# A fused four-layer cross-attention kernel: the Mamba block's heads computed with channels on partitions, its squares summed on TensorE, and the batches' stages merged in another order

## The reference, cut to what matters

```python
zxbcdt = _rms(x, norm_w) @ in_proj_w
z = zxbcdt[..., :D_INNER]                       # D_INNER = 512
xBC = zxbcdt[..., D_INNER:D_INNER + CONV_DIM]   # 768 channels
dt = jax.nn.softplus(zxbcdt[..., -H_M:] + dt_bias)
...                                             # conv over 4 taps, then silu
xh = xBC[..., :D_INNER].reshape(b, L, H_M, HEADDIM)   # 8 heads of 64
...                                             # scan over the tokens gives ys
y = ys.transpose(1, 0, 2, 3) + D_skip[None, None, :, None] * xh
u = _rms(y.reshape(b, L, D_INNER) * jax.nn.silu(z), gnorm_w)
return resid + u @ out_proj_w
```

## Time and profile before

| | |
|---|---|
| median of 3 runs | 1412.81 us (1411.97 to 1413.31) |
| the profiled execution | 1414.21 us |
| its span, first to last instruction | 1411.0 us |
| mean granted clock of TensorE | 0.956 |
| TensorE busy with products | 1261.4 us, 89% |
| TensorE busy with weight loads | 996.6 us, 71% |
| VectorE | 959.5 us, 68% |
| ScalarE | 783.4 us, 56% |
| POOL | 339.1 us, 24% |

### The profile page before, as it was taken

The page is one execution under the profiler, slowest core; times in us unless marked ns, Lnnn a source line. Parts: engine busy times, 40 slices in busy tenths (PEclk is TensorE's granted clock), DMA queues, the critical chain, the costliest instruction groups (busy, mean ns, idle before and its releaser), DMA issues.

```text
span 1411.0 us, 25836 instructions
## 1 busy us (share of the span) xinstructions
PE 1261.4 (89%) x9426; PEld 996.6 (71%) x9426; DVE 959.5 (68%) x1877; ACT 783.4 (56%) x2690; POOL 339.1 (24%) x766
## 2 busy tenths in 40 slices
PE   3567889999999999999999999999999999988755
PEld 2345667877787887877787778788787778766633
DVE  2355466969687877868696968777786869583522
ACT  1124364857565666757475756566675847464411
POOL 0101313231322232232323132223223232302020
PEclk9779999999999999999999999999999999999755
DMA  6901010100001010101000000101010100000000
GB/s 200 331 1 41 1 42 1 34 16 19 29 0 48 0 48 0 45 4 45 4 25 23 15 33 0 48 0 48 0 45 4 45 4 11 27 5 4 4 4 4
DMA packets 28586, 44.38 MB, mean 31 GB/s; under 512 B 4710, under 2 KB 20614, under 8 KB 28044
## 3 DMA queue, kind: packets, MB, share of 16 engines
q1 hardware_dynamic: 26252, 31.41, 7.0%
q0 software_dynamic: 2304, 12.58, 2.5%
HBM read 37.65 MB, written 6.34 MB: 31 GB/s over the span
## 4 chain that ended last, share of the span: by engine, by line
PE 64%; DVE 21%; ACT 11%; issue 2%; DMA 1%; POOL 1%; SPq 0%; POOLq 0%; DVEq 0%; ACTq 0%
PE psum L487 43%; PE psum L481 7%; ACT A L790 5%; ACT sa_p L790 4%; DVE small_ L1003 4%; PE psum L642 3%; PE psum L535 3%; PE psum L694 2%; PE psum L706 2%; PE psum L661 2%; DVE A L997 2%; DVE sa_p L1011 1%; DVE sa_p L997 1%; PE psum L551 1%; DVE A L1088 1%
## 5 line engine op out<-in xcount | busy, mean ns | idle before, releaser
L1279 POOL TENSOR_SCALAR small_<-small_ 128x1 f32<-128x1 f32 x112 | 37.1, 331 | 865.3 <-ACT A L908 382.5
L790 ACT ACTIVATE A<-A,small_ 128x128 f32<-128x128 f32 x384 | 148.6, 393 | 86.0 <-DVE small_ L1004 86.0
L481 PE MATMUL psum<-cst,A 128*128 128x128 f32 x672 | 108.3, 288 | 64.4 <-DVE A L1011 27.0
L783 ACT ACTIVATE A<-psum 128x1024 f32<-128x1024 f32 (+2 forms) x112 | 77.1, 688 | 156.9 <-PE psum L481 109.1
L481 PEld LDWEIGHTS psum<-cst,A 128*128 128x128 f32 x672 | 80.3, 147 | 101.4 <-DVE A L1011 40.5
L1168 DVE SCALAR_TENSOR_TENSOR A<-psum,half_cw,A 128x127 f32<-128x127 f32 (+2 forms) x288 | 75.2, 343 | 41.1 <-ACT A L894 41.1
L790 ACT ACTIVATE sa_p<-sa_p,small_ 128x128 f32<-128x128 f32 x256 | 99.1, 397 | 4.4 <-DVE small_ L1004 4.4
L790 ACT ACTIVATE ca_p<-ca_p,small_ 128x128 f32<-128x128 f32 x256 | 98.7, 391 | 4.8 <-DVE small_ L1004 4.8
L1010 DVE RECIPROCAL small_<-small_ 128x8 f32<-128x8 f32 x112 | 22.3, 199 | 91.1 <-ACT A L790 81.5
L997 DVE TENSOR_TENSOR A<-psum,cst 128x1024 f32<-128x1024 f32 x32 | 39.2, 1225 | 56.9 <-PE psum L535 56.9
L790 ACT ACTIVATION_READ_ACCUMULATOR A<-A,small_ 128x1 f32 x384 | 73.8, 192 | 0.0
(11 more groups left out here) (217 smaller groups left out, 3213.6 us busy)
## 6 DMA issues: line engine op xcount, KB each, us to landing
inT<-in_tokT SPq DMA_DIRECT2D x16, 256.0 KB, 2.9
kv_rows<-A SPq DMA_DIRECT2D x16, 256.0 KB
ctx_in<-in_ctx SPq DMA_DIRECT2D x16, 128.0 KB, 2.1
A<-bias_rows SPq DMA_DIRECT2D x1, 2048.0 KB, 9.3
Wsakv<-in_wsa_kv SPq DMA_DIRECT2D x1, 2048.0 KB, 12.7
Wcakv<-in_wca_kv SPq DMA_DIRECT2D x1, 2048.0 KB, 14.0
ctx_end<-in_tokT SPq DMA_DIRECT2D x16, 128.0 KB, 2.2
out<-x_out SPq DMA_DIRECT2D x16, 128.0 KB, 1.7
```

Of the source, the lines that this page charges most:

```text
L481: mm = pe.transpose(out[:, c * P:(c + 1) * P], src[:, c * P:(c + 1) * P], ident)
L783: return act.activation(out, in_, ACT.Copy)
L790: ins = act.activation(p[:, h * T:(h + 1) * T], p[:, h * T:(h + 1) * T], ACT.Exp, bias=sm(part, "nm", w * HU + h, w * HU + h + 1), accum_o ...
L1279: then(pool.tensor_scalar(t, src, scale, eps, ALU.mult, ALU.add))
```

## The change

z is computed with channels on partitions. Each head has its `dbx` as the stationary operand (64 columns) and its mask as the moving one, so that two heads share 128 partitions, one in each half, and the result has channels on partitions. The skip becomes four operations that take `xbcT` and a column of D_skip. The gated result is then in the form that `m_out` wants as stationary operand; `m_back` and `m_uT` are gone. The sum of the squares over the channels is now over partitions: a new stage `m_sq` multiplies the squares with a column of ones, into the first column of `Pd`; VectorE's `m_mean` scales it, and POOL takes the root. `kv3` waits for `m_mean` (`m_ms`), since it writes the same bank. All four orders are rewritten.

```diff
 ORDER = {
-    "PE": "314312434231314134232121413142443143142142321424141",
-    "Activation": "434342134314141232113441323142123242441",
-    "DVE": "412121431444342134133214314442124124134111241",
-    "Pool": "4244141121132",
+    "PE": "314312434231314134234121241214431434124131232421414",
+    "Activation": "43432413431414123142132123143123422414",
+    "DVE": "4121231414443421341433213241444214121441113214",
+    "Pool": "4324144211112",
 }
@@ m_dtz (PE)
-                product(Pd, split(xnT3), rows_of(Wmi, 0, DI)).then_inc(sem["m_z"], 1)
+                product_T(Pd, Wmi, 0, DI // P, split(xnT3)).then_inc(sem["m_z"], 1)
@@ m_heads (PE)
                 for h in range(HM):
-                    mm = pe.matmul(Pc[:, h * HDM:(h + 1) * HDM], aV[:, h * T:(h + 1) * T], dbx[:, h * HDM:(h + 1) * HDM],
+                    c, e = h // 2, HDM * (h % 2)
+                    mm = pe.matmul(Pc[e:e + HDM, c * T:(c + 1) * T], dbx[:, h * HDM:(h + 1) * HDM], aV[:, h * T:(h + 1) * T],
                                    start=True, stop=True)
@@ (PE)
-            def m_back(t):
+            def m_sq(t):
+                need(t, "m_gssq")
+                ones = C("upto")[:, T - 1:T]
+                product(Pd[:, 0:1], split(junk3, DI // P), [ones] * (DI // P)).then_inc(sem["m_sq"], 1)
+
+            def m_out(t):
                 need(t, "m_g")
-                turn(Pd, gated, DI // P).then_inc(sem["m_uT"], 1)
-
-            def m_out(t):
-                need(t, "m_uT_sb")
-                product(Pc[:, 0:D], split(uT, DI // P), rows_of(Wmo, 0, D)).then_inc(sem["m_o"], 1)
+                product(Pc[:, 0:D], split(gated, DI // P), rows_of(Wmo, 0, D)).then_inc(sem["m_o"], 1)
@@ kv3 (PE)
+                need(t, "m_ms")
@@ (ACT)
-                act.activation(junk3, gated, ACT.Square, accum_out=sm(4, "ssq1")).then_inc(sem["m_gssq"], 1)
-
-            def m_uT(t):
-                need(t, "m_uT")
-                copy(uT, Pd).then_inc(sem["m_uT_sb"], 1)
+                act.activation(junk3, gated, ACT.Square).then_inc(sem["m_gssq"], 1)
@@ m_mix (DVE)
-                dve.tensor_tensor(heads(xD, HM), xh, each(pr("D_skip"), HDM), ALU.mult)
@@ m_gated (DVE)
-                then(dve.tensor_tensor(gated, xD, Pc, ALU.add))
+                for c in range(DI // P):
+                    at = slice(c * T, (c + 1) * T)
+                    ins = dve.scalar_tensor_tensor(gated[:, at], xbcT[:, at], pc("D_skip", c), Pc[:, at], ALU.mult, ALU.add)
+                then(ins)
@@ (DVE)
+            def m_mean(t):
+                need(t, "m_sq")
+                dve.tensor_scalar(sm(4, "ssq1"), Pd[:, 0:1], 1.0 / DI, 1e-5, ALU.mult, ALU.add).then_inc(sem["m_ms"], 1)
@@ m_grms (POOL)
-                need(t, "m_gssq")
-                rsqrt(4, sm(4, "r1"), sm(4, "ssq1"), 1.0 / DI, 1e-5, "m_grstd")
+                need(t, "m_ms")
+                pool.tensor_tensor(sm(4, "r1"), sm(4, "ssq1"), neg_half[:, 0:1], ALU.pow).then_inc(sem["m_grstd"], 1)
```

More of the change, by code:

```diff
@@ L42 @@
          ("ca_g", KD), ("ca_b", KD), ("ca_cg", KD), ("ca_cb", KD),
-         ("m_w", KD), ("gn_w", DI // P), ("conv_w", CC * TAPS), ("conv_b", CC), ("ln_w", KD), ("ln_b", KD)]
-_ROWS = [("rms_w", D), ("sa_bo", D), ("ca_bo", D), ("bv", HD0), ("dt_bias", HM), ("A_log", HM), ("D_skip", HM)]
+         ("m_w", KD), ("gn_w", DI // P), ("conv_w", CC * TAPS), ("conv_b", CC), ("D_skip", DI // P), ("ln_w", KD), ("ln_b", KD)]
+_ROWS = [("rms_w", D), ("sa_bo", D), ("ca_bo", D), ("bv", HD0), ("dt_bias", HM), ("A_log", HM)]
 def _places(parts):
@@ L106 @@
 PART4 = ["m_squares", "m_hat", "m_dtz", "m_xbc", "m_tap0", "m_tap1", "m_tap2", "m_tap3", "m_silu", "m_seg", "m_xh", "m_heads",
-         "m_back", "m_out", "kv3", "hat3", "q3", "c3_s", "c3_p", "c3_m", "c3_out"]
+         "m_sq", "m_out", "kv3", "hat3", "q3", "c3_s", "c3_p", "c3_m", "c3_out"]
 PARTS = {1: PART1, 2: PART2, 3: PART3, 4: PART4}
@@ L145 @@
     "sa_hatT", "sa_q", "sa_k", "sa_v", "sa_oT", "sa_y", "ca_cT", "ca_hatT", "ca_q", "ca_k", "ca_v", "ca_oT", "ca_y",
-    "m_hatT", "m_dt", "m_z", "m_xbc", "m_seg", "m_xhG", "m_y", "m_uT", "m_o", "c3_hatT", "c3_q", "c3_kv", "c3_oT", "c3_y",
+    "m_hatT", "m_dt", "m_z", "m_xbc", "m_seg", "m_xhG", "m_y", "m_sq", "m_o", "c3_hatT", "c3_q", "c3_kv", "c3_oT", "c3_y",
     "l0_osb", "gate_th", "out0_ssq", "x1_ssq", "kv1_sb", "o1T_sb",
     "sa_xnT", "sa_k_sb", "sa_v_sb", "sa_oT_sb", "ca_cnT", "ca_xnT", "ca_k_sb", "ca_v_sb", "ca_oT_sb",
-    "m_ssq", "m_xT", "m_acc", "m_th", "m_thz", "m_u", "m_E", "m_gssq", "m_uT_sb", "c3_xnT", "c3_oT_sb",
+    "m_ssq", "m_xT", "m_acc", "m_th", "m_thz", "m_u", "m_E", "m_gssq", "c3_xnT", "c3_oT_sb",
     "ctx_var", "cn_hat", "bk0", "q0_sb", "attnT_sb", "out0T", "y0", "x1", "x1gT", "q1_sb", "o1", "x2",
     "sa_var", "sa_hat", "sa_q_sb", "xa", "ca_var", "ca_hat", "ca_q_sb",
-    "x4", "m_hat", "m_dtp", "m_conv", "m_xs", "m_sz", "m_M", "m_g", "c3_var", "c3_hat", "c3_q_sb", "c3_bk", "x6",
+    "x4", "m_hat", "m_dtp", "m_conv", "m_xs", "m_sz", "m_M", "m_g", "m_ms", "c3_var", "c3_hat", "c3_q_sb", "c3_bk", "x6",
     "ctx_rstd", "out0_rstd", "x1_rstd", "near_at", "sa_rstd", "ca_rstd", "m_rstd", "m_grstd", "c3_rstd",
@@ L248, in build @@
         xnT3, hat3, aV, probs3 = at4[3][:, 0:D], at4[3][:, D:2 * D], at4[3], at4[3]
-        sz, uT, v3, q3 = at4[4][:, 0:DI], at4[4][:, DI:2 * DI], at4[4][:, 0:D], at4[4][:, D:2 * D]
-        thz, xD, dbx, bk3 = at4[5][:, 0:DI], at4[5][:, 0:DI], at4[5][:, DI:2 * DI], at4[5]
+        sz, v3, q3 = at4[4][:, 0:DI], at4[4][:, 0:D], at4[4][:, D:2 * D]
+        thz, dbx, bk3 = at4[5][:, 0:DI], at4[5][:, DI:2 * DI], at4[5]
         pad_at = PB2["ca"][:, 0:T].bitcast(I32)
@@ L767, in _ @@
                 "m_hat": [m_turn], "m_dtz": [m_dtz], "m_xbc": [m_xbc], "m_seg": [m_seg], "m_xh": [m_xh],
-                "m_heads": [m_heads], "m_back": [m_back], "m_out": [m_out], "kv3": [kv3], "hat3": [turn3], "q3": [query3],
+                "m_heads": [m_heads], "m_sq": [m_sq], "m_out": [m_out], "kv3": [kv3], "hat3": [turn3], "q3": [query3],
                 "c3_s": [scores3], "c3_p": [turn_probs3], "c3_m": [mix3], "c3_out": [project3],
@@ L931, in _ @@
                 "m_squares": [m_squares], "m_hat": [m_norm], "m_dtz": [m_gate], "m_tap0": [m_last_tap], "m_tap3": [m_tanh],
-                "m_seg": [m_decay], "m_heads": [m_gsquares], "m_back": [m_uT], "hat3": [norm3],
+                "m_seg": [m_decay], "m_heads": [m_gsquares], "hat3": [norm3],
                 "c3_s": [lambda t: softmax(t, "c3", 0, probs3)], "c3_p": [turned3], "c3_m": [mixed3],
@@ L1233, in _ @@
                 "m_silu": [m_silu],
-                "m_xh": [m_mix], "m_heads": [m_gated], "m_out": [result_m], "kv3": [keys_values3], "hat3": [normed3],
+                "m_xh": [m_mix], "m_heads": [m_gated], "m_sq": [m_mean], "m_out": [result_m], "kv3": [keys_values3], "hat3": [normed3],
                 "q3": [query3], "c3_s": [lambda t: softmax_max(t, "c3", 0, probs3, P_4, spread(pad_add[:], HU))],
@@ L1390, in _ @@
                 "fold1": [fold1], "fold4": [fold4],
-                "m_squares": [m_rms], "m_xbc": [m_steps], "m_heads": [m_grms], "m_out": [deviation3],
+                "m_squares": [m_rms], "m_xbc": [m_steps], "m_sq": [m_grms], "m_out": [deviation3],
             }
@@ L1409, in layouts @@
         f["L3_xattn_conv_w"].reshape(CC, P, TAPS).transpose(1, 0, 2).reshape(P, CC * TAPS), down(f["L3_xattn_conv_b"]),
+        down(np.repeat(f["L3_xattn_D_skip"], HDM)),
         down(f["L3_xattn_ca_ln_w"]), down(f["L3_xattn_ca_ln_b"])], axis=1)
     rows = np.concatenate([f["L0_xattn_rms_w"], f["L2_xattn_sa_bo"], f["L2_xattn_ca_bo"], f["L0_xattn_bv"], f["L3_xattn_dt_bias"],
-                           f["L3_xattn_A_log"], f["L3_xattn_D_skip"]])
+                           f["L3_xattn_A_log"]])
     order = [2 * (4 * w + c) + e for w in range(2) for e in range(2) for c in range(4)]
```

## The result

The changed kernel takes 1422.04 us (median of 4 runs, 1420.64 to 1423.9) against 1412.39 of the kernel before (4 runs, 1411.59 to 1413.31): a ratio of 1.0069, 95% interval 1.0051 to 1.0086. It is slower by 9.6 us. Its profiled execution took 1423.9 us with a span of 1422.1, which is 11.1 more than before. That execution is the slowest of the four, 1.9 us above their median.

A forecast was written before the change was run, and what follows sets the result against it. The prediction took TensorE to bound the loop's turn, VectorE close behind, and a chain over several engines the ends. Span 1411.0 + 7.2 (13 turns) - 2.5 - 4.5 = 1411.2, forecast 1413.0 us, range 1401 to 1423.

The forecast's parts named there:

- The likeliest case: Whole kernel: a longer turn and shorter ends cancel, 1413.0 us, range 1408 to 1418, chance 0.42.
- rival B: POOL's queue: the centering's root y0 comes late, +0.5 to 0.6 us a turn, 1421 us, chance 0.17.
- 77.6: Length in us of a loop turn above which the prediction would be wrong, by POOL's queue or non-overlapping heads.
- the ends: Stretches outside the 13 loop turns: forecast -2.5 us ahead of the loop and -4.5 behind it.
- The work of TensorE: TensorE per loop turn: z +0.08, heads -0.85, m_back -0.53, m_sq +0.75, sum -0.55 us.
- Steps 1 to 6: TensorE's waits ahead of m_heads, l0_p1, sa_s0, gate0, kv3, hat3 in the new order: 3.2 us a turn in all.
- the ledger: The prediction's stepping of the new order's stages through a turn, with c3_hat ready for hat3 at 655.86.
- The waits that go: Old waits ahead of 661.07, turn_o1 and kv0, late in a turn, vanish: gain 1.55 us a turn.
- Behind the loop: Last three turns, a chain over several engines: -1.2, -1.7 and -1.6 us, sum -4.5, between -8 and -1.
- Ahead of the loop: Turns before the loop: near_q earlier, so the gather's chain starts sooner, -2.5 us, between -5 and +1.
- rival C: Heads in column halves don't overlap, records stay at 0.115 us, 0.85 a turn lost: 1427 us, chance 0.03.

The follow-up runs named there:

- sixth run: Changed kernel with POOL's near_rows earlier and pass_on later, m_heads behind sa_v and several other stages moved: 1398.59 us, ratio 0.9905.
- eighth run: Changed kernel with only one of m_sq's four products (2 records in place of 8): 1423.19 us, ratio 1.0074.
- fourth run: Changed kernel with the mean moved on VectorE ahead of ca_p1 and sa_s1: 1422.21 us, ratio 1.0058.
- third run: Changed kernel with POOL's order alone altered, near_rows ahead of m_sq and pass_on behind back0: 1414.51 us, ratio 1.0006.
- first run: Changed kernel's arithmetic in the old kernel's order, m_sq in m_back's place: 1420.1 us, ratio 1.0042.
- fifth: Changed kernel's arithmetic in the old order, m_sq behind sa_s1 on TensorE, the mean behind gate0 on VectorE: 1409.72 us, ratio 0.9987.
- second: Kernel before with the new order alone, old arithmetic, m_back in m_sq's place: 1464.87 us, ratio 1.0346.
- seventh run: Kernel before with the new order and old arithmetic, VectorE's D_skip product left out: 1435.41 us, ratio 1.0176.

## Why the prediction was right in its range and not in its figure

The time lies inside the range of 1401 to 1423, with 1 us to spare, and 9 us above the figure of 1413. The likeliest case, no difference, was not what came: rival B was, 1421 in the text, with a chance of 0.17, and the turn of 77.70 is over the 77.6 that the prediction named as its sign. That B's 1421 is within 1 us of the median is in part luck: the ends gave back 3.5 and not the 7 forecast, and the trace that this is read from is 1.9 above the median.

- **The work of TensorE**, -0.55 forecast, is -0.36: heads -0.82 (1.02 in the sixth run's timeline, for 1.84), m_back -0.53, z +0.07, and m_sq +0.92 (648.58 to 649.50), not 0.75. The mis-sized term is m_sq: I took the row with 16 moving columns, at 0.09 a record, and it cost the 0.115 of a full one, my upper bound. It didn't reach the time: the eighth run shows that it lies beside VectorE's softmax. Two slips in the working did no harm: z's 1.83 less 1.78 is +0.05, not +0.08, and 16 records in 1.04 less the tail are 0.88, not 0.95.
- **The order's waits.** Steps 1 to 6 of the prediction say 1.2, 0.4, 0.3, 0.5, 0.35 and 0.45. The trace has 1.05, 0.28, none printed (0.18 between the end of l0_m1 and sa_s0), 0.23, 0.34 and 0.35, with the tails of about 0.16 on top of the printed ones at most places; the five printed ones are put down to the VectorE lines that were named. Where the fourth is smaller, m_sq's undersized 0.17 goes into it. hat3 starts 55.33 us after kv0; the ledger had 55.34. That kv3's new wait and hat3's are one chain, the fourth run shows.
- **The waits that go.** The idle times of the earlier trace rows ahead of 661.07, of turn_o1 and of kv0 are gone, as forecast.
- **What failed** is the sentence of rival B that y0 could start "at 657.2", 0.36 ahead of need, which the figure took as covered: for the moves in POOL's queue the sum had nothing. Moved to the turn shown, 657.2 is 662.6; y0 started at 663.59 and center0, free at 663.56, waited 0.41 and the tail. Two operations of POOL ran long in this chain, not one, by 0.42 and 1.06 over the 0.55 and 0.24 that they take elsewhere, in each of the 13 turns. The third run takes the queue apart and gets 0.73 a turn back, 9.5 us in 13 turns; each against the runs of the kernel before beside it, the loss falls from 9.65 us to 0.82. With 0.6 for this the forecast of a turn, 77.05 to 77.1, comes to the 77.70 that was measured. I had the mechanism, the place and the point from which it decides, and gave it 0.17, because I took the long operations for accidents of a few turns. They repeat in each turn, and the trace of the kernel before had their pattern already (below).
- **The ends.** Behind the loop I forecast -4.5: x_out to x_out the three turns gained 1.1, 1.6 and 2.15, which is 4.8 (forecast 1.2, 1.7 and 1.6). But c3_out now stands behind out1, so the first x_out comes 0.95 behind x2 where it came 0.77 ahead. This 1.7 is paid once and was in no term. Ahead of the loop I forecast -2.5 and got -0.4. But these are single executions: in the changed kernel and in the fourth and eighth runs, whose order differs from its in the mean alone and not at all, x2 came at 216.82, 215.56 and 219.57, and from the last x2 to the end they took 195.5, 193.4 and 195.7. Of the term ahead nothing is shown, and the one behind is known to about 2 us.
- **That heads overlap in column halves** (rival C the other way): 16 records in 1.02. The Trainium skill's "TensorE: Matmul & The Clock Gate", "The mechanism", lets weight loads overlap only across row groups, and here the rows are the same; the measurement decides against it. In the rows with 512 moving columns a record takes 0.44 (sa_v, 3.54 for 8), which is 0.11 for 128 columns, and the heads, with 128 moving columns, take 0.064 each: products in the two halves overlap. The same page, "LDWEIGHTS (loading the stationary operand)", gives columns by 1.2 GHz, 0.107 for 128: eight make an estimate of 0.85 for m_sq. The 0.92 measured agrees better with it than with my 0.75.

Is the order or the arithmetic to blame? Both, and neither alone. In the old order the arithmetic costs 0.47 a turn (first run), because m_sq hangs on ScalarE too; one stage later it costs nothing (fifth). The new order with the old arithmetic costs 2 us a turn and more (second). The two together cost 1.18, of which 0.73 are POOL's queue (third). The rest is the order's waits for VectorE: the sixth run, with m_heads behind sa_v and several other moves, takes 0.79 a turn less than the third. That m_heads came too early is the likeliest reading of it; a run with that move alone was not made.

## What to carry to other kernels

When an order of stages written by hand changes, step the changed stretch on all engines with the durations of the trace: the chain came out to a few hundredths of a microsecond. Then look for the places with little to spare, and at what the other engines do beside them: five small POOL operations took 1.5 us more than the sum of their usual times beside VectorE's work on operands outside PSUM, and a slack of 0.36 us behind them was none. In this loop an operation that was long in one turn was long in nearly all, so a long one can be priced. A stage that needs one engine more than the stage whose place it takes (m_sq for m_back) wants another place, and a cheaper product counts only where TensorE doesn't wait on both sides of it.

## What the runs showed of the hardware that was not expected

**POOL.** POOL's long operations aren't accidents, and they don't belong to a place in its queue. In the loop turns of all ten traces, 520 POOL operations ran over 0.15 us longer than the shortest of their kind. Each of them began while VectorE was in a tensor_tensor with both operands outside PSUM, and none ended ahead of it: most ended 0.05 to 0.1 us behind it, a copy 0.25 and the powers 0.4 to 0.6. Only 14 others began beside such a one and stayed short. Beside VectorE's other operations, nearly all of which read PSUM or have a single tensor operand, 1803 began, and none was long.

The kernel before shows it too, VectorE above and POOL below, where the same line takes 0.19 undisturbed:
```profile
659.79 1.22 DVE L1011 TENSOR_TENSOR sa_p<-sa_p,small_ 128x1024 f32<-128x1024 f32 x1
```
```profile
660.12 0.95 POOL L1279 TENSOR_SCALAR small_<-small_ 128x1 f32<-128x1 f32 x1 [4.59 <-ACT A L834]
```

The third run moved two POOL operations, one out from beside such a VectorE operation and one in, and their times changed with it. No run moved VectorE's.

**The clock.** The granted clock fell to 0.50 behind an idle time of 1.66 us in the last four turns of the second run, for a shorter time in two others, and not in the seven turns of 78.6 us with the same idle. In the seventh run it fell behind one of 1.06 in the first turn and in three others, each third one. A turn costs 3.3 us more where it fell as in the last four, and 1.7 in the seventh run.
